# Value products of an attention kernel, issued for four key tiles together in every fourth unit

## The reference

```python
scores = einsum('bqhd,bkhd->bhqk', q, k) * scale    # plus the mask that adj gives
attn   = softmax(scores, axis=-1)
out    = einsum('bhqk,bkhd->bqhd', attn, v).reshape(b, n, d) @ Wo + bo
```

## Time and profile before

| | us |
|---|---|
| median of 3 runs (lowest, highest) | 3125.32 (3124.43, 3125.84) |
| span of the profiled execution | 3120.2 |
| PE busy | 3039.6 |
| DVE busy | 2430.3 |
| ACT busy | 2135.5 |
| transposes L739, PE busy | 1132.0 |
| scores L727, PE busy | 737.1 |
| value products L758, PE busy | 658.4 |

### The profile page before, as it was taken

The page is one execution under the profiler, slowest core; times in us unless marked ns, Lnnn a source line. Parts: engine busy times, 40 slices in busy tenths (PEclk is TensorE's granted clock), DMA queues, the critical chain, the costliest instruction groups (busy, mean ns, idle before and its releaser), DMA issues.

```text
span 3120.2 us, 64907 instructions
## 1 busy us (share of the span) xinstructions
PE 3039.6 (97%) x23872; PEld 2162.3 (69%) x23872; DVE 2430.3 (78%) x4427; ACT 2135.5 (68%) x3794; POOL 590.0 (19%) x538
## 2 busy tenths in 40 slices
PE   7999997999999999999999999999999999999999
PEld 6888886667666666666676667676767666666666
DVE  6776766888787878787878888877778787878776
ACT  3000005888787878787778777887878787878887
POOL 2222220114040405050413223010101010102000
PEclk9999998999999999999999999999999999999999
DMA  3101104232222323233223242323232222323232
GB/s 118 48 17 46 55 14 104 55 82 69 73 66 72 80 53 89 62 76 70 71 62 89 77 113 62 89 62 89 62 86 65 69 69 60 91 52 85 65 72 55
DMA packets 123648, 217.86 MB, mean 70 GB/s; under 512 B 20017, under 2 KB 88241, under 8 KB 123313
## 3 DMA queue, kind: packets, MB, share of 16 engines
q1 hardware_dynamic: 122160, 209.14, 27.0%
q0 software_dynamic: 1152, 4.19, 0.4%
HBM read 53.87 MB, written 25.17 MB: 25 GB/s over the span
## 4 chain that ended last, share of the span: by engine, by line
PE 82%; issue 1%; DVE 1%; DMA 0%; ACT 0%; POOL 0%; DVEq 0%; ACTq 0%; POOLq 0%
PE t_pt_ps L739 34%; PE t_ot_ps L758 19%; PE t_s_ps L727 15%; PE t_g_ps L713 4%; PE t_g_ps L712 4%; PE t_g_ps L714 4%; PE t_g_ps L779 1%; PE t_g_ps L783 1%; PE t_g_ps L798 1%; DMA mask<-in_adj 0%; DVE t_T L945 0%; DVE t_w_lo L1045 0%; ACT t_T L876 0%; PE t_pt_ps L712 0%; PE t_pt_ps L714 0%
## 5 line engine op out<-in xcount | busy, mean ns | idle before, releaser
L945 DVE CUSTOM_DVE_ANT_0 t_T<-t_s_ps,mask 128x1024 f32<-128x1024 f32 x1024 | 1246.0, 1217 | 237.9 <-PE t_s_ps L727 230.2
L876 ACT ACTIVATE t_T<-t_T,t_low 128x1024 f32<-128x1024 f32 x1024 | 1177.8, 1150 | 54.7 <-DVE t_low L945 40.5
L739 PEld LDWEIGHTS t_pt_ps<-t_ident,t_T 128*128 128x128 f32 x8192 | 887.8, 142 | 434.4 <-issue 389.3
L739 PE MATMUL t_pt_ps<-t_ident,t_T 128*128 128x128 f32 x8192 | 1132.0, 282 | 7.5 <-DVE t_PT L1020 6.3
L881 ACT ACTIVATE t_PT<-t_pt_ps 128x512 f32<-128x512 f32 x1324 | 757.8, 596 | 427.0 <-PE t_pt_ps L739 426.6
L727 PE MATMUL t_s_ps<-t_k,t_q 128*128 128x512 f32 x2048 | 737.1, 441 | 34.3 <-issue 30.3
L758 PE MATMUL t_ot_ps<-t_PT,shared 128*32 128x256 f32 x8192 | 658.4, 394 | 0.3 <-ACT t_PT L881 0.2
L1020 DVE COPY t_PT<-t_pt_ps 128x512 f32<-128x512 f32 x724 | 500.1, 691 | 175.0 <-PE t_pt_ps L739 162.2
L758 PEld LDWEIGHTS t_ot_ps<-t_PT,shared 128*32 128x32 f32 x8192 | 162.6, 108 | 311.9 <-issue 274.2
L727 PEld LDWEIGHTS t_s_ps<-t_k,t_q 128*128 128x128 f32 x2048 | 313.6, 194 | 37.4 <-issue 34.2
L255 ACT ACTIVATE g_yT_hi<-g_ps 128x512 fp32r<-128x512 f32 x64 | 38.3, 598 | 401.1 <-PE g_ps L195 401.1
(11 more groups left out here) (185 smaller groups left out, 3160.6 us busy)
## 6 DMA issues: line engine op xcount, KB each, us to landing
t_q<-t_st_hi SPq DMA_DIRECT2D x256, 128.0 KB, 2.3
t_k<-t_st_hi SPq DMA_DIRECT2D x256, 128.0 KB, 2.4
t_k<-t_st_lo SPq DMA_DIRECT2D x256, 128.0 KB, 2.4
t_q<-t_st_lo SPq DMA_DIRECT2D x256, 128.0 KB, 2.4
shared<-x_after_graph_layers SPq DMA_DIRECT2D x8, 1024.0 KB, 8.0
t_xe<-x_after_graph_layers SPq DMA_DIRECT2D x32, 256.0 KB, 3.7
x_after_layer<-t_xe SPq DMA_DIRECT2D x32, 256.0 KB, 2.2
shared<-x_after_layer SPq DMA_DIRECT2D x8, 1024.0 KB, 6.5
```

Of the source, the lines that this page charges most:

```text
L739: last = nc.tensor.transpose(pt_ps[half][:, i * P:(i + 1) * P], T[u % RING][:, kt * P:(kt + 1) * P], ident[:])
L876: nc.scalar.activation(T[u % RING][:], T[u % RING][:], ACT.Exp, bias=low[:, u % RING:u % RING + 1], scale=-1.0, accum_out=rsum[:, u:u + 1] ...
L945: nc.vector.tensor_tensor_reduce(out=T[u % RING][:], in0=s_ps[u % 2][:], in1=mask[:, qt, :], scale=1.0, scalar=3.4e38, op0=ALU.add, op1=AL ...
```

## The change

`values` of four key tiles are issued together in every fourth unit (u % 4 = 0), ahead of the transposes of that unit, in place of one key tile in each unit. ACT's `copy_ot`, which takes the sum when a pair of heads is full, moves from unit 7 of each 16 to unit 5, since the last of its products now stands in unit 4. Nothing is computed otherwise, and the number of instructions that do work is the same.

```diff
--- before.py
+++ after.py
@@ -420,6 +420,7 @@
 
 
 UNITS = 64
+GROUP = 4
 EARLY = [(9, ("norm", 3)), (11, ("turn", 0)), (13, ("out", 0)), (15, ("turn", 1)), (17, ("out", 1)),
          (26, ("turn", 2)), (28, ("out", 2)), (30, ("turn", 3)), (32, ("out", 3))]
 MID = [(18, ("qk", 1, 0, 0)), (20, ("qk", 1, 1, 0)), (22, ("qk", 1, 0, 1)), (24, ("qk", 1, 1, 1)),
@@ -824,8 +825,9 @@
 
                             pe.wait_ge(ot_done, 4 * job + what[1] + 1 if what[1] < 3 else 4 * job)
                         one_block(block_at(job, k), what, lay, job + 1)
-                    if u >= NT or before is not None:
-                        values(job, u)
+                    if u % GROUP == 0 and (u >= NT or before is not None):
+                        for w in range(u, u + GROUP):
+                            values(job, w)
                     transposes(job, u)
 
             pe.wait_ge(made, 3)
@@ -907,8 +909,8 @@
                 for u in range(UNITS):
                     if u + 1 < UNITS or after is not None:
                         exp(job, u + 1)
-                    if u % (2 * NT) == NT - 1 and (u >= NT or before is not None):
-                        copy_ot(UNITS * job + u + 1 - NT)
+                    if u % (2 * NT) == NT - GROUP + 1 and (u >= NT or before is not None):
+                        copy_ot(UNITS * job + u + GROUP - 1 - NT)
                     halves = (0, 1) if u in scalar_halves(table) else (0,)
                     copy_first = u in table and table[u][1][0] in SHORT
                     if copy_first:
```

## The result

| | before | after |
|---|---|---|
| median (lowest to highest), 8 runs each | 3122.80 (3120.87 to 3125.84) | 3113.84 (3112.17 to 3116.37) |
| span of the profiled execution | 3120.2 | 3112.4 |

The ratio of the times is 0.997, with a 95% interval of 0.996 to 0.998: the change makes the kernel 9 us faster, 0.3%, clear of the measurement's uncertainty and far from the 180 us that PE alone would save by the prediction's sum.

The account below looks back on a forecast made before the run. The prediction took PE's own stream as the bound, with DVE and ACT close behind; group gains and losses summed to +0.20 us per job, 3 us in all, giving 3128 us, range 3080 to 3172 (the forecast's own 3103 to 3153).

Parts of the forecast that it names:

- the sum over the sixteen groups: Over one job's groups of four units, six gain 2.24 us and ten lose 2.44: +0.20 per job, 3 us in all.
- the wait of the burst for ACT's copy: At units 0, 8 and 16 the value products also wait for ACT's copy of the unit before: 0.14 to 0.18 us.
- the low part of a qk on DVE: In groups with qk blocks, DVE's low part starts 2.31 us after the block and takes 0.79 before the copy.
- PE's saving: Fewer passages into and out of value products save PE 0.71 us per group of four, 180 us over 254 groups.
- The chain of DVE: In a plain group DVE's copies and masked sums behind the burst set the length: T(0) + 5.78, or 8.29 us.
- The chain of ACT: ACT's copies and exps behind the burst, with a double copy or copy_ot, make a group last about T(0) + 5.98 us.
- The signs on record: Trace signs: products 0.43 apart, S to T 0.54, PE busy 91 to 93%, copy waits 0.5 to 0.7 us per group, DVE idle 1.6.
- Only the gains hold: DVE and ACT enter groups further ahead, so the ten losing groups come out even: 36 us less, 3090; chance 0.18.
- PE stays the bound: PE's stream sets the time everywhere, so its whole saving comes out: 180 us less, 2945; chance 0.07.
- ACT late at the heads: At head starts the burst waits for ACT, pushed back 0.3 us at each of 128 heads: 38 us added, 3167; chance 0.20.

Follow-up runs that it names:

- g2: The change with bursts of two key tiles in every second unit instead of four in every fourth: 3035.15 us, ratio 0.9716 to the kernel before.
- g8_ot7: The change with bursts of eight key tiles, copy_ot left in unit 7 of 16: 3153.75 us, ratio 1.0091 to the kernel before.
- g4_long: The changed kernel with the products of two of each four tiles issued twice: 3333.3 us, ratio 1.0671 to the kernel before.
- g4_light: The changed kernel with DVE's masked sum and ACT's exp over half of the keys: 2994.99 us, ratio 0.9599 to the kernel before.
- g4_ot7: The changed kernel with copy_ot back at unit 7 of 16: 3116.03 us, ratio 0.9976 to the kernel before.

## Why the prediction was right and wrong

The forecast was 3128 us, 3 above the 3125.3 of the kernel before, with 0.42 for slower and 0.38 for faster. The kernel became 9 us faster. The mechanism was right, the sign was wrong, and the time lies inside the range. The step that failed is the sum over the sixteen groups, in the size of its terms. The two largest errors are the wait of the burst for ACT's copy, taken as 0.14 to 0.18 and measured as 0.02 to 0.10, and the low part of a qk on DVE, taken as 0.79 and measured as 0.67.

- **PE's saving: right, and a little more.** 1.86 from the burst's start to T(0), as in the rows above. A transpose group that doesn't follow value products is quicker than I had it, though:

```profile
2081.41 1.04 PE L740 MATMUL t_pt_ps<-t_ident,t_T 128*128 128x128 f32 x8
...
2082.20 0.71 PE L728 MATMUL t_s_ps<-t_k,t_q 128*128 128x512 f32 x2
```

T to the next S is 0.79, not the 0.85 of the earlier trace rows. The passage out of V also slows the first transpose behind it, and I had read T's length in a unit with V. It counts where PE is the bound, up to 3 x 0.06 in the group of unit 44. PE alone would so save 8.26 - 7.35 = 0.91 in a plain group, not 0.71.

- **The chain of DVE: right.** T(0) + 5.78 in the plain group (its terms as listed add up to 5.77), DVE idle 1.60 behind the burst, and g2, g8_ot7 and g4_long came out as this chain has them, g2 with 0.11 more per pair of units for the hand-over of banks.
- **The chain of ACT: right.** The groups of units 4, 28 and 60 were given 8.48, 9.90 and 8.92; they took 8.48, 9.88 and 8.91.
- **The signs on record.** Further products in a row, S to T, DVE's 1.6 and the lengths of the groups came as told. PE's busy share is 94%, not 91 to 93%, and its waits for copies are 59.3 us, 0.23 per group, not 0.5 to 0.7: the profile counts much of the waiting as busy, as the plain group above shows.
- **The sum over the sixteen groups: this step failed, on sizes.** It adds sixteen small differences of both signs, and its result of +0.20 us per job is far smaller than what their errors add up to. By the starts of S, in jobs without a loop's boundary, forecast and measured: unit 0 8.43, 8.34; 4 8.48, 8.48; 8 8.85, 8.70; 12 9.51, 9.61; 16 11.16, 10.85; 20 11.15, 10.97; 24 10.31, 10.19; 28 9.90, 9.88; 32 10.39, 10.36; 36 9.33, 9.32; 40 9.43, 9.39; 44 11.81, 11.68; 48 11.08, 11.02; 52 11.37, 11.26; 56 9.69, 9.67; 60 8.92, 8.91. The sum is 1.18 less than forecast, -0.98 per job in place of +0.20. No group is off by more than 0.31 in 11, but fifteen of sixteen are off to one side or not at all.

Two terms make about half of it. The first is the wait of the burst for ACT's copy at units 0, 8 and 16, taken as 0.14 to 0.18: V started 0.66, 0.70 and 0.70 to 0.74 after S (medians over the jobs), so 0.02 to 0.10 over the undisturbed 0.64, and some 0.25 of the 1.18 lies here. I had used 0.74 for the way from the start of ACT's copy to the work that waits for it, which holds for T. The second is the low part of a qk on DVE, at unit 16:

```profile
2010.48 0.39 PE L713 MATMUL t_g_ps<-t_hT_hi,t_w_hi 128*128 128x512 f32 x1
...
2012.79 0.75 DVE L965 SCALAR_TENSOR_TENSOR t_st_lo<-t_g_ps,t_b_qk,t_st_hi 128x512 fp32r<-128x512 f32 x1 [0.77 <-ACT t_st_hi L868]
...
2013.46 0.68 DVE L1022 COPY t_PT<-t_pt_ps 128x512 f32<-128x512 f32 x1
```

The low part starts 2.31 after the block, as taken, but the copy follows 0.67 after it (2012.79 to 2013.46), not 0.79. The 0.79 was the least distance in the kernel before, where the copy was always waiting for the transposes. It stands in the groups of units 16, 20 and 52, 0.36 together. Some 0.1 more are slips of the sum itself: by their own terms the groups of units 16, 24 and 52 come to 0.02 less than stated, the one of unit 44 to 12.49 - 0.71 = 11.78 and not 11.81, and PE's own need in a plain group to T(0) + 5.02, not 5.04 (which enters no group). The rest is spread over the other groups, about 0.1 at most in one.

Of the span, the 255 stretches of four units whose start and end the trace has sum to 12.7 us less, and the two ends are longer by 4.9: together 7.8 less. The part ahead of the third S was 2.2 longer in this execution. The change does not touch it, and in the fourteen traces of the kernels told of here it ends anywhere from 508.1 to 513.1 us, so this is scatter. The tail is 2.7 longer. Of it 1.2 stands in the last four units, of which three have no value products now. The other 1.5 is the clock: of the output products behind them, which the change does not touch, the first ones ran from 3100.34 to 3103.67 at a granted clock of 0.52, mostly its lower level of 1.2 GHz, and in the kernel before at 1.00.

- **The rivals.** "Only the gains hold" had the sign, with 3090, but not the mechanism: the groups of units 4, 24, 36, 40, 52 and 60 do lose 0.1 to 0.6 each. "PE stays the bound" is refuted by the windows, and its 180 us by g4_light even where DVE and ACT are relieved. ACT late at the heads did not happen in the change (V at most 0.10 late, in the medians); it did in g4_ot7, 0.53 at unit 8.
- **The chances.** The forecast's own range allowed 0.1 of error per group in one direction, 25 us, and the error was 0.07. That part was sized rightly; what I should have drawn from it is that the sign of a 3 us sum carried nothing, and "same" or "slower" deserved no lead over "faster". Of the 14 us between forecast and result, 2.5 are the lower median of the kernel before over eight runs, 3122.8 for 3125.3.

## What to carry to other kernels

Grouping work on the engine that is the bound saves its passages, but every other engine whose work waits behind the group may run dry meanwhile (DVE for 1.60 us of a burst of 1.86 here), and must make that up before the next one. Compare, per period, the bound's shortened stream with (end of the burst + the others' serial chain to the point where the bound waits for them), and choose the longest burst that keeps the first one the greater. Of the lengths tried here (1, 2, 4 and 8) that was two tiles, and four only in the group whose three long blocks keep PE busy anyway. Count one-bank hand-overs among the chains: they are what keeps two tiles at 7.87 in place of 7.64. When a forecast is a sum of many small terms of both signs, give its sign no more weight than the common error of its terms allows.

## What the runs showed of the hardware

- A passage of PE from full-width products to ones with 32 columns of stationary operand and back costs at three places: 0.10 us ahead of the value products, 0.14 behind them (0.57 for the last ones, 0.43 in a row), and 0.06 in the first transposes (0.85, and 0.79 where no value products stood ahead). The third I had not expected.
- Handing one bank from T to a copy and back to T costs more than the copy lasts: the next T starts 0.74 after the copy's start, the copy lasting 0.60 on ACT and 0.69 on DVE. So the units without value products in plain groups of the two-tile and of the relieved kernel took 1.44 us from S to S (medians) with 1.33 of PE's own work, even with DVE and ACT relieved.
- The granted clock can be lower in one execution than in another over the same work: 0.52 for 3.3 us in the tail of the kernel after, 1.00 in that of the kernel before. PE had waited much the same ahead of it in both, 0.72, 1.07 and 1.05 us against 0.72, 1.07 and 1.06. What set it off isn't shown. In the plain groups, with about 1.0 of 8.34 us of waiting, the clock shown is 1.00.
